# A decoder kernel's first feed-forward stage: PE's turning of the Silu's rows, DVE's order and recurrence's inputs are moved by a slot

## What is computed

```python
def _L0_ffn_ref(x, w1, conv_w, conv_b, w2):
    h = bit_linear(x, w1)                       # 256 -> 1024, weights rounded to -1, 0, 1, rows to 8 bits
    h = depthwise_conv1d(h.transpose(0, 2, 1), conv_w, conv_b).transpose(0, 2, 1)   # 3 taps over tokens
    h = jax.nn.silu(h)
    return bit_linear(h, w2)                    # 1024 -> 256: each row scaled by its largest magnitude
x = _layernorm(x + _L0_ffn_ref(x, ...))
# layer 1: Bu = x @ B_w.T + B_b, and over the 1024 tokens of each batch, one after the other:
state = jnp.tanh(state * Aexp + bu_t)
```

## Time and profile before

| what | value |
|---|---|
| median of 3 runs | 2505.74 us (2503.68 to 2508.46) |
| the profiled execution | 2505.45 us |
| its span, first to last instruction | 2503.4 us |
| PE, DVE, ACT, POOL busy | 1849.5, 1900.6, 1337.7, 801.1 us |
| layer 0's feed-forward stage | about 1123 to 1566 us |

### The profile page before, as it was taken

How to read it: one execution, slowest core, us unless ns; L and a number is a source line. 1 busy time by engine, 2 the same in 40 slices (tenths; PEclk the granted TensorE clock), 3 DMA queues, 4 the chain that set the end, 5 groups by cost and what they waited for, 6 DMA issues and landing times. The chain is left out here.

```text
span 2503.4 us, 35555 instructions
## 1 busy us (share of the span) xinstructions
PE 1849.5 (74%) x11696; PEld 1181.1 (47%) x11696; DVE 1900.6 (76%) x4634; ACT 1337.7 (53%) x3303; POOL 801.1 (32%) x889
## 2 busy tenths in 40 slices
PE   8849999999658888874555554785999999344555
PEld 4413333333346776763444443453777767133333
DVE  4678888887358888878999997433666665599998
ACT  2106666667313433430688889649888852133333
POOL 2510000000026346423333331002633643355553
PEclk9959999999779999996766666677999999667666
DMA  2011111110010100000000000200000000000000
GB/s 73 17 27 29 30 29 28 30 30 17 22 43 11 30 11 10 11 1 1 1 1 1 1 1 1 65 1 17 1 18 1 1 1 1 32 13 13 13 13 17
DMA packets 42805, 41.50 MB, mean 17 GB/s; under 512 B 16054, under 2 KB 34670, under 8 KB 42622
## 3 DMA queue, kind: packets, MB, share of 16 engines
q1 hardware_dynamic: 42622, 39.23, 5.9%
HBM read 22.03 MB, written 4.19 MB: 10 GB/s over the span
## 5 line engine op out<-in xcount | busy, mean ns | idle before, releaser
L763 ACT ACTIVATE ST<-ST,aexp 128x1 f32<-128x1 f32 x2046 | 582.7, 374 | 53.5 <-PEq L57 53.5
L597 ACT ACTIVATE PT<-PS 128x512 f32<-128x512 f32 x576 | 309.8, 597 | 219.3 <-PE PS L482 188.2
L558 DVE CUSTOM_DVE_ANT_0 junk<-PS,maskw 128x128 bf16<-128x128 f32 (+3 forms) x512 | 226.4, 486 | 33.8 <-PE PS L459 33.8
L459 PE MATMUL PS<-KT,QT 48*128 48x512 bf16 (+3 forms) x768 | 190.2, 351 | 54.1 <-DMA QT<-QS 33.0
L94 PE MATMUL PS<-ident,X 128*128 128x128 f32 x320 | 76.3, 326 | 188.3 <-DVE X L128 171.0
L94 PE MATMUL PS<-ident,j_t 128*128 128x128 f32 x320 | 77.1, 426 | 165.6 <-ACT j_t L1800 136.6
L561 DVE TENSOR_REDUCE MX<-PS 128x1 f32<-128x512 f32 x256 | 164.6, 684 | 27.7 <-PE PS L459 24.8
L501 PE MATMUL PS<-PT,VP 128*32 128x256 f32 (+1 forms) x2560 | 184.2, 370 | 0.0
L1561 PE MATMUL PS<-L_xattn_VW,l_pT 112*128 112x256 f32 x704 | 159.4, 382 | 9.3 <-DVE i_xb L1587 6.5
L123 POOL TENSOR_TENSOR n_rs<-n_ve,neghalf 128x1 f32<-128x1 f32 x96 | 110.3, 1165 | 153.4 <-DVE n_ve L118 153.4
L459 PEld LDWEIGHTS PS<-KT,QT 48*128 48x128 bf16 x768 | 58.5, 94 | 199.9 <-issue 80.4
(11 more groups left out here) (297 smaller groups left out, 4500.4 us busy)
## 6 DMA issues: line engine op xcount, KB each, us to landing
KT<-KS SPq DMA_DIRECT2D x192, 32.0 KB, 2.0
QT<-QS SPq DMA_DIRECT2D x192, 32.0 KB, 2.0
xs<-in_x SPq DMA_DIRECT2D x8, 512.0 KB
cx<-in_x SPq DMA_DIRECT2D x32, 128.0 KB, 2.0
out<-j_xn SPq DMA_DIRECT2D x32, 128.0 KB, 1.7
QT<-NMT SPq DMA_DIRECT2D x192, 2.0 KB
f_raw<-in_L_ffn_w SPq DMA_DIRECT2D x2, 1024.0 KB, 5.2
j_raw<-in_L_ffn_w SPq DMA_DIRECT2D x2, 1024.0 KB, 5.1
```

The source lines that it names most:

```text
L459: T.matmul(bank(u % 3)[:, 0:w * P], QT[i % R][rows, qt * P:(qt + 1) * P], KT[i % R][rows, k0 * P:(k0 + w) * P], start=True, stop=True).the ...
L558: V.tensor_tensor_reduce(junk[u % 3][:, 0:w * P], bank(u % 3)[:, 0:w * P], maskw[:, BANK - w * P:], 1.0, NEG, ALU.add, ALU.max, MX[i % 2][ ...
L597: C.activation(PT[n % 4][:, 2 * pr + e, 0:w], bank(3 + u % 3)[:, 0:w], ACT.Exp, scale=0.25).then_inc(e_done, 1)
L763: C.activation(self.ST[:, m, t:t + 1], self.ST[:, m, t - 1:t] if t else self.zero[:, :], ACT.Tanh, bias=self.BU[:, m, t:t + 1], scale=self ...
```

## The change

PE's loop turns the Silu's rows of tile b = j - 2 instead of j - 3, behind the turning of X's rows and ahead of the product with B. On DVE the largest magnitude (of the same tile c as before) comes first in the slot, then the writing of recurrence's inputs, now of tile e = j - 5, then the copy of hqT. The loops of DVE and ACT have one more slot, and recurrence's steps start in slot 9.

```diff
--- before.py
+++ after.py
@@ -1345,17 +1345,12 @@
 
         def pe():
             for j in range(NT + 4):
-                a, c, d = j, j - 3, j - 4
+                a, b, d = j, j - 2, j - 4
                 if on(d):
                     T.wait_ge(f_hq, d + 1)
                     if d >= 1:
                         T.wait_ge(f_hqT, d)
                     transposes(hq[d % 2], bank(6).bitcast(BF16), KH).then_inc(f_hqtr, 1)
-                if on(c):
-                    T.wait_ge(f_silu, c + 1)
-                    if c >= 1:
-                        T.wait_ge(qF.scaled_done, c)
-                    transposes(g[c % 2][:, :, :].rearrange("p k n -> p (k n)"), bank(4, 2), KH).then_inc(f_gtr, 1)
                 if on(d):
                     T.wait_ge(f_hqT, d + 1)
                     if d >= 1:
@@ -1377,6 +1372,12 @@
                     if d >= 1:
                         T.wait_ge(R.fed, d)
                     transposes(X[:, d, :], bank(3), KD).then_inc(f_xtr, 1)
+                if on(b):
+                    T.wait_ge(f_silu, b + 1)
+                    if b >= 1:
+                        T.wait_ge(qF.scaled_done, b)
+                    transposes(g[b % 2][:, :, :].rearrange("p k n -> p (k n)"), bank(4, 2), KH).then_inc(f_gtr, 1)
+                if on(d):
                     T.wait_ge(f_xT, d + 1)
                     for k in range(KD):
                         last = T.matmul(bank(3)[rows(d), D:D + P], R.BwT[:, k, :], xT[d % 2][:, k * P:(k + 1) * P],
@@ -1394,16 +1395,20 @@
                                                   src[i % 2][:, q, :], ALU.mult, ALU.add)
                 return last
 
-            for j in range(NT + 4):
-                a, b, c, d = j, j - 2, j - 3, j - 4
+            for j in range(NT + 5):
+                a, b, c, d, e = j, j - 2, j - 3, j - 4, j - 5
+                if on(c):
+                    V.wait_ge(f_gtr, c + 1)
+                    qF.dve_max(c, bank(4, 2))
+                if on(e):
+                    V.wait_ge(f_bmm, e + 1)
+                    V.tensor_scalar(R.BU[rows(e), (e % B) // 2, (e // B) * P:(e // B) * P + P], bank(3)[rows(e), D:D + P],
+                                    R.bb[rows(e), :], None, ALU.add).then_inc(R.fed, 1)
                 if on(d):
                     V.wait_ge(f_hqtr, d + 1)
                     if d >= 2:
                         V.wait_ge(f_mm2, d - 1)
                     V.tensor_copy(hqT[d % 2][:, :], bank(6).bitcast(BF16)).then_inc(f_hqT, 1)
-                if on(c):
-                    V.wait_ge(f_gtr, c + 1)
-                    qF.dve_max(c, bank(4, 2))
                 if on(b):
                     V.wait_ge(f_cC, b + 1)
                     if b >= 2:
@@ -1444,22 +1449,18 @@
                         last = V.tensor_mul(h[a % 3][:, q0:q0 + k, :], bank(q0 // 3)[:, 0:k * HW].rearrange("p (j n) -> p j n", j=k),
                                             rs.unsqueeze(1).broadcast_to([P, k, HW]))
                     last.then_inc(f_h, 1)
-                if on(d):
-                    V.wait_ge(f_bmm, d + 1)
-                    V.tensor_scalar(R.BU[rows(d), (d % B) // 2, (d // B) * P:(d // B) * P + P], bank(3)[rows(d), D:D + P],
-                                    R.bb[rows(d), :], None, ALU.add).then_inc(R.fed, 1)
                 if on(c):
                     V.tensor_scalar(ds[c % 4][:, :], qF.amax[c % 4][:, :], w2.scale[:, :], None, ALU.mult).then_inc(f_ds, 1)
 
         def act():
-            for j in range(NT + 4):
+            for j in range(NT + 5):
                 b = j - 2
-                if j >= 8:
+                if j >= 9:
                     R.act_states(9)
                 if on(b):
                     C.wait_ge(f_cR, b + 1)
                     C.activation(g[b % 2][:, :, :], g[b % 2][:, :, :], ACT.Silu).then_inc(f_silu, 1)
-                if j >= 8:
+                if j >= 9:
                     R.act_states(9)
 
         def pool():
```

## The result

The changed kernel takes 2515.44 us (median of 6 runs, 2514.7 to 2518.82), the kernel before 2507.1 us on the same chips (6 runs, 2503.68 to 2509.88). The ratio is 1.0036, with a 95% interval from 1.0023 to 1.0049: slower by 0.36%, some 9 us.

| stretch of the span | before, us | changed, us |
|---|---|---|
| up to layer 0's feed-forward stage | 1123.33 | 1124.77 |
| that stage, to the next stage's first DMA | 442.68 | 451.79 |
| of it, behind the last Silu | 25.84 | 35.87 |
| the keys of the next stage | 53.68 | 56.22 |
| the rest | 883.7 | 883.9 |

What follows compares the result with a forecast made beforehand. Steady slots were bound by h, POOL's two passes and the taps, the stage's end by ACT's recurrence steps. 10.04 - 0.82 - 0.26 = +8.96 us on 2505.45, plus 0.29 for the runs' median, gave 2514.7 us, range 2509.5 to 2517.5.

Steps and rivals of the forecast that it cites:

- The PE wait is not on the path: In the steady slot, attacking L140's 26.5 us wait for PE's transposes gains 0.00 us; y still comes every 13.03 us.
- The taps stand for POOL: The first tap's eight DVE instructions are held by POOL's second pass: 2.80 us, against 2.18 where POOL is idle.
- Who is held: Skill's rule: two-SBUF-input DVE and SBUF-reading GpSimd instructions exclude each other, issue order deciding; an earlier tap only stands longer.
- The length of the first taps: In the steady slot on DVE, the first tap's eight instructions grow from 2.80 us to about 3.7.
- A new wait at the copy of hqT: On DVE, the copy waits about 0.2 us for hq's transposes on PE, in place of the old 0.83 us wait.
- One tap slips in at the start: In the first slot with w2's tail (1152 us), one tap runs between POOL's two passes, saving 0.26 us.
- The late slot without POOL: In the slot of 1532 us, POOL has nothing left; taps start about 1532.7 instead of 1533.54, 0.82 us sooner.
- both terms: Savings in the first slot with w2's tail and the slot of 1532 us: 0.26 + 0.82 = 1.08 us.
- ACT's tail: Behind the last Silu, 126 activations instead of 90 hold up the barrier before the next stage: +10.04 us.
- A: Rival: taps get ahead of POOL's second pass and keep DVE's turn; y 1.49 us sooner in 28 slots, 2473 us; 6%.
- B: Rival: one tap slips in before POOL's second pass in each slot, 28 x 0.26 = 7.3 us, 2507.4 us; 8%.
- C: Rival: PE's chain, over 1.7 us late, bounds each slot; 2.2 us late would be 14 us more, 2529 us; 4%.

## Why the prediction was right, point by point

- **The PE wait is not on the path.** Shown. y to y stayed at 13.03 us while L140's wait fell by 22.5 us. Without POOL's second pass the same edit brings 18.8 us in the stage.
- **The taps stand for POOL.** Shown by the two kernels without that pass (2.18 us) and by the second taps, which became the ones that stand (2.84 us) when the pass was moved onto them.
- **Who is held.** The rule of the Trainium skill's page "SBUF — State Buffer", section "Who interferes with whom", weighed in the prediction, has two halves. With the first, that an instruction with two SBUF inputs stands for a GpSimd one that reads SBUF, these runs agree. For the second, that the one issued first holds the other, they give small signs only, since every tap is short. In the kernel with the pass behind the first taps, one tap began at 1138.17, POOL's pass at 1138.28, and the pass took 1.99 us, the longest of all, against its usual 1.89 to 1.91. The one tap that got ahead in the changed kernel ran from 1155.83 to 1156.17, and POOL's second pass began at 1156.03 and kept its 1.89 us. In the kernel with the pass behind the second taps the normalization ran until 1312.13, and the pass began at 1311.95 and took 1.93 us. So whether the normalization kept its 0.41 us because it was issued first, or because it hardly competes with POOL at all, stays open.
- **The length of the first taps.** One size was off: the first taps took 3.29 to 3.47 us in most slots and not about 3.7, since they were ready later than I had put it. One slot has the forecast's figure: with a wait of 0.11 us at the copy the taps took 3.73 us, and y still came after 13.03.
- **A new wait at the copy of hqT.** It is there, but mostly 0.29 to 0.43 us and not 0.2: PE began g's rows 0.15 us after the scaling's end instead of 0.06 (1321.01 against 1319.59 + 1.27 = 1320.86), and their place on PE was 1.87 us (1321.01 to 1322.88), which I had put at 1.71. It costs nothing beside POOL, so the sum was not hurt.
- **One tap slips in at the start.** In the first slot with w2's tail the first tap was issued at 1155.83, before POOL's first pass ended (1154.05 + 1.91 = 1155.96), and took its usual 0.34 us; the second stood for the second pass, the two together for 2.25 us. From the stage's start to the first y it is 34.80 us instead of 35.05: 0.25 us, predicted 0.26.
- **The late slot without POOL.** The last Silu ended 415.91 us after the stage's start instead of 416.83, 0.92 us sooner for both terms, predicted 1.08.
- **ACT's tail.** 35.13 - 25.10 = 10.03 us, predicted 10.04. The stage became 9.11 us longer, predicted 8.96.
- **The whole time.** 2515.44 us, predicted 2514.7. The mechanism and its terms held, but so close a figure is partly luck: over its six runs the kernel before is at 2507.1 us and not at the 2505.74 that I had added to, and the medians are 8.3 us apart and not 8.96.
- **The rivals.** A (the taps keep POOL out) did not happen: in the slot shown they come 0.47 us after POOL's second pass began. Once a semaphore put them first, the time fell, to the extent that the pass met nothing else; that is A's gain and not its mechanism, for no run has a row of taps that keeps POOL out by itself, and after the one tap that got ahead the next stood for the whole pass. B needed a start before that pass, which one slot had, the first; C needed a lateness of PE of 1.7 us, which was not seen.

## What to carry to other kernels

Before a wait is removed, ask what its engine does next and whether that has to stand anyway: here the work behind the attacked wait was done 0.8 us before the moment at which POOL let DVE go (1325.04 against 1325.86 in the earlier trace rows). A slot in which the wait happened to be short answers the question without a run. And when a step is moved by one slot, count what each other engine starts or ends with it; a chain of dependent small steps at the end of a stage is paid in full, as long as no other engine's tail is longer. What the same steps cost in the next stage's idle time these runs do not settle, since that part also varies with TensorE's clock.

## What the runs showed of the hardware beyond the prediction

A DVE instruction that depends on the one just ahead started 0.12 us later than an independent one in its place, which speaks for an order that interleaves two tiles' chains. And f32 to bf16 from SBUF to SBUF with one input, the rounding, also stood for POOL's pass: it took 0.86 us instead of 0.68. The Trainium skill, page "SBUF — State Buffer", section "Who interferes with whom", says that `tensor_scalar`, which the rounding is, can contend with GpSimd when its operands allow a mode that uses both of VectorE's ports; the row agrees. I had expected it, at twice the price.
